# Six batches instead of five in the second group norm, the last bias additions on DVE, and new hand-written orders, in a fused convolution and attention kernel

## The chip, the cores and the metric

One core of a Trainium2 chip runs the whole program. The metric is the device time of one execution in microseconds (us). Names of engines: PE is TensorE (PEld its weight loads), DVE is VectorE, ACT is ScalarE, POOL is GpSimd, SP is SyncE, which here only issues DMAs.

## What is computed

The input x has 8 images of 128 channels and 16 x 16 pixels, all float32. The reference, cut to what matters:

```python
# stage 0, per channel
out = x + bias[None, :, None, None]
out = upsample2(out, up_filter * 2)              # separable, 12 taps, both axes
out = leaky_relu(out, 0.2) * sqrt(2)
y   = downsample2(out, down_filter)              # back to 16 x 16
# stage 1
xn  = group_norm(y, gn1_gamma, gn1_beta, 32)
q, k, v = split(qkv_w @ xn + qkv_b)              # 8 heads of 16
a   = softmax(q @ k.T / 4) @ v                   # 256 x 256 scores per head
a   = out_w @ a + out_b
a   = group_norm(a, gn2_gamma, gn2_beta, 32)
h, g = split(mlp1_w @ a)                         # 512 rows each
return y + mlp2_w @ (silu(h) * g)
```

Both group norms are taken per image, so each image's norm needs that image alone.

## The kernel before

Each of the five engines has its own straight list of steps, written out by hand, in blocks named after it. A step waits for counters (semaphores) that other engines raise, and an engine goes through its list in order, so a step that waits holds everything behind it on its engine. Nothing is scheduled at run time. Products that need float32 accuracy in one fast pass are done as three passes over a high and a low part (`three`, lines 772 to 774).

The steps that the change and the prediction touch:

- **Stage 0.** SP loads the input as windows `win` in three parts: two quarters of the batch (`in_xw`, 6 windows each of 128 x 256) and then the second half (`in_xh`, 6 windows of 128 x 512). `add_bias` adds the bias to a window in place, on DVE (line 1499) for the quarters and on POOL (line 364) for the half. PE's `upsample(n)`, n from 0 to 15, makes a quarter of the enlarged picture of two images (line 790), ACT's `leaky(n)` reads it (line 507), PE's `downsample(b)` makes image b of y (line 822) and ACT's `read_y(b)` takes its squares and sums (lines 515, 517). Upsample n needs `leaky(n - 4)`, since four PSUM banks are shared. ACT also blanks the six stacks of q and k once (`fill`, line 500, 1.9 us each).
- **First norm.** `GN1_BATCHES` has three batches of images. Of each, PE sums (`group_means`, line 806), DVE makes the variance (lines 1514 to 1517), POOL the coefficients (`first_coefficients`, lines 378 to 381), and POOL normalises image by image (`normalise`, lines 405 to 410); image 0 is done by DVE (lines 1523 to 1526).
- **Attention, image by image.** PE's `project_qk(i)` and `project_v(i)`; ACT and DVE split q and k in parts (`high_parts`, lines 524 and 525; `low_parts`, line 1531); SP copies them with six DMAs into the stacks (`stack(i)`, line 311). PE's `maxima(i, h, c)` (line 862) makes scores from which DVE's `reduce_max(i, h)` (line 1548) takes row maxima; `turn_maxima(i)` turns them, ACT's `read_rows(i)` reads them, and SP's `rows(i)` (line 317) copies them in as a row. Then PE's `scores(i, h, c)` (line 888), ACT's `exponentials(i, h)` (line 531), PE's `weigh` (line 913, 32 matmuls an image), and a chain that normalises and projects: `read_sums`, `merge`, `turn_sums`, `invert`, `spread_inverse`, `turn_inverse`, `normalise`, `project_out`, `read_proj`, `square_attn`.
- **Second norm.** `GN2_BATCHES` is [(0, 2), (2, 4), (4, 6), (6, 7), (7, 8)]. For each batch: `group_means` on PE, `read_means` on DVE (line 1505), `second_coefficients` on POOL (lines 388 to 394), then `second_norm(i)` on POOL (lines 447 to 452).
- **MLP.** Each image has two pairs p. PE's `up_project(p, j, e)` (four calls a pair, three matmuls each), ACT's `squash(p)` (line 598, from p = 8 on line 600 with another function), DVE's `swish_value` and `gate` (lines 1580, 1597, 1593), ACT's `split_high(p)` (line 586), POOL's `split_low(p)` (line 424), PE's `down_project(p, e)` (two calls a pair, three matmuls each), DVE's `residual(i)` (line 1602), SP's `store(i)` (line 322).

PE's list mixes all of this: maxima run one to two images ahead of scores, and MLP calls are put between them.

Of the kernel before, what the change touches and what calls it, by code (L numbers as in the profile page):

```python
# [75 lines left out]
GN2_BATCHES = [(0, 2), (2, 4), (4, 6), (6, 7), (7, 8)]  # L76
# [4 lines left out]
def build(nc, xw, xh, factors, vecs, wqk, wv, wo, w1, w2,  # L81
          ident, gmat, swap, out):
    ctx = ExitStack()
    with ctx:
# [131 lines left out]
        biased_dve, biased_pool = sem("biased_dve"), sem("biased_pool")  # L216
# [65 lines left out]
        def _(sp):  # L282
# [51 lines left out]
            stack(5)  # L334
            stack(6)
            rows(4)
            rows(5)
            stack(7)
            rows(6)
            store(0)  # L340
            store(1)
            rows(7)
# [6 lines left out]
        def _(pool):  # L349
# [9 lines left out]

            def add_bias(t):  # L360
                pool.wait_ge(fac_in, 16)
                pool.wait_ge(win_in[t][2], 16)
                x4 = win_at(t, 2, 2).rearrange("p (b c) -> p b c", c=C)
                pool.tensor_tensor(x4, x4, bias_bc[:, None, :].to_broadcast([128, B // 2, C]), ALU.add).then_inc(biased_pool, 1)  # L364
# [90 lines left out]
            for j in range(0, 5):  # L455
                add_bias(j)
# [3 lines left out]
            add_bias(5)  # L460
            first_coefficients(1)
            normalise(2)
            normalise(3)
            split_w2()
            split_w1()
            first_coefficients(2)
# [3 lines left out]
            second_norm(0)  # L470
            second_norm(1)
            split_low(0)
            second_coefficients(4)
            second_norm(2)
            second_norm(3)
            for j in range(1, 4):
                split_low(j)
            second_coefficients(5)
            second_norm(4)
            split_low(4)  # L480
            split_low(5)
            second_norm(5)
            split_low(6)
            second_coefficients(6)
            second_norm(6)
            for j in range(7, 10):
                split_low(j)
            second_coefficients(7)
            split_low(10)
# [5 lines left out]
        def _(act):  # L495
# [116 lines left out]
            leaky(6)  # L612
            fill(2, 0)
            for j in range(7, 10):
                leaky(j)
            read_y(2)
            high_parts(0)
            leaky(10)
            fill(2, 1)
            read_y(3)  # L620
            read_early_v(0)
# [4 lines left out]
            read_y(4)  # L626
            read_early_v(1)
            leaky(15)
            high_parts(2)
            read_y(5)  # L630
            read_y(6)
            read_rows(0)
            read_y(7)
            read_early_v(2)
            sum_biases()
            exponentials(0, 0)
            exponentials(0, 1)
            high_parts(3)
            for j in range(2, 6):
                exponentials(0, j)  # L640
            read_rows(1)
            exponentials(0, 6)
# [6 lines left out]
            exponentials(1, 2)  # L649
            spread_inverse(0)  # L650
            for j in range(3, 6):
                exponentials(1, j)
            read_rows(2)
            read_proj(0)
            exponentials(1, 6)
            square_attn(0)
            exponentials(1, 7)
            read_sums(1)
            exponentials(2, 0)
            exponentials(2, 1)  # L660
            high_parts(5)
            spread_inverse(1)
            for j in range(2, 6):
                exponentials(2, j)
            read_proj(1)
            read_rows(3)
            square_attn(1)
            exponentials(2, 6)
            exponentials(2, 7)
            read_sums(2)  # L670
            exponentials(3, 0)
            exponentials(3, 1)
            high_parts(6)
            exponentials(3, 2)
            exponentials(3, 3)
            spread_inverse(2)
            for j in range(4, 7):
                exponentials(3, j)
            read_rows(4)
            exponentials(3, 7)  # L680
            squash(0)
            read_proj(2)
            square_attn(2)
            read_sums(3)
            split_high(0)
            high_parts(7)
            exponentials(4, 0)
            spread_inverse(3)
            squash(1)
            for j in range(1, 4):  # L690
                exponentials(4, j)
            read_proj(3)
# [3 lines left out]
            square_attn(3)  # L696
            exponentials(4, 6)
            exponentials(4, 7)
            split_high(1)
            squash(2)  # L700
# [3 lines left out]
            exponentials(5, 2)  # L704
            exponentials(5, 3)
            split_high(2)
            exponentials(5, 4)
            spread_inverse(4)
            exponentials(5, 5)
            exponentials(5, 6)  # L710
            read_rows(6)
            exponentials(5, 7)
            squash(3)
            read_proj(4)
            square_attn(4)
            split_high(3)
            read_sums(5)
            exponentials(6, 0)
            exponentials(6, 1)
            squash(4)  # L720
            exponentials(6, 2)
            spread_inverse(5)
            for j in range(3, 6):
                exponentials(6, j)
            read_proj(5)
            exponentials(6, 6)
            square_attn(5)
            exponentials(6, 7)
            split_high(4)
            squash(5)  # L730
            read_rows(7)
            split_high(5)
            read_sums(6)
            exponentials(7, 0)
            squash(6)
            exponentials(7, 1)
            exponentials(7, 2)
            spread_inverse(6)
            exponentials(7, 3)
# [730 lines left out]
        def _(dve):  # L1470
# [269 lines left out]
            for j in range(11, 14):  # L1740
                gate(j)
# [68 lines left out]
```

## Time and profile before

| | us |
|---|---|
| median of 3 runs (146.26 to 147.64) | 147.03 |
| the profiled execution, its own time | 146.93 |
| span of the profiled execution | 145.1 |
| PE busy | 138.5 (95%) |
| ACT busy | 104.5 (72%) |
| DVE busy | 88.2 (61%) |
| POOL busy | 75.2 (52%) |

The clock that PE was granted is 1.0 of full speed (2.4 GHz) in all 40 slices of the page. A busy time counts from start to modelled end of overlapping instructions, so it overstates: what an engine can do per microsecond is read from starts of instructions that follow each other without a wait.

### The profile page before, as it was taken

Reading aid. Unit: us, or ns where it says so; the run is one execution under the profiler, and the core shown is the slowest. Engines: PE = TensorE matmul, PEld = TensorE weight load, DVE = VectorE, ACT = ScalarE, POOL = GpSimd, SP = SyncE. Lnnn points to the kernel's source line nnn. Section 1 sums busy time; section 2 is a strip of 40 time slices with the busy share of each in tenths; the row PEclk is TensorE's granted clock in tenths of the full one; section 3 lists DMA queues with packets and bytes.
Section 4 is the critical chain, followed back from the end, with each engine's and each line's share of the span. In section 5 each row is a group of like instructions: output and inputs, shape, how many; then the busy total and the mean of one; then the engine's idle time right before and its main releaser. Section 6 shows DMA issues by size and latency. Waiting matters only on the chain.

```text
span 145.1 us, 3307 instructions
## 1 busy us (share of the span) xinstructions
PE 138.5 (95%) x1150; PEld 122.2 (84%) x1150; DVE 88.2 (61%) x187; ACT 104.5 (72%) x235; POOL 75.2 (52%) x126
## 2 busy tenths in 40 slices
PE   6999888999999999999999999999999999999992
PEld 5899578999988687788896998797997997999891
DVE  1940133077649679699699889768684715634251
ACT  6956997955448688697793996894995995766330
POOL 7008985066584850402840304892108988589930
PEclk9999999999999999999999999999999999999999
DMA  3999200746530061331606103501001010011012
GB/s 110 285 272 338 91 0 15 205 113 185 178 113 0 10 169 49 106 113 42 182 0 175 53 0 85 138 0 38 0 7 38 0 43 0 0 41 36 0 36 72
DMA packets 12368, 12.12 MB, mean 83 GB/s; under 512 B 1600, under 2 KB 11328, under 8 KB 12352
## 3 DMA queue, kind: packets, MB, share of 16 engines
q1 hardware_dynamic: 12208, 11.81, 27.4%
q8 instruction: 9, 0.15, 0.4%
q10 hardware_dynamic: 144, 0.10, 0.2%
q14 instruction: 7, 0.06, 0.1%
HBM read 4.50 MB, written 1.05 MB: 38 GB/s over the span
## 4 chain that ended last, share of the span: by engine, by line
PE 63%; SPq 10%; POOL 9%; DMA 7%; issue 4%; DVE 3%; POOLq 1%; ACT 1%; ACTq 0%
PE ps L888 10%; PE po L913 10%; PE pm L862 9%; SPq L311 6%; SPq L286 4%; DMA win<-in_xh 4%; PE pf L772 3%; PE pf L774 3%; PE pf L773 3%; PE px L772 3%; POOL gated_lo L424 3%; PE po L936 3%; PE px L774 2%; PE px L773 2%; POOL win L364 2%
## 5 line engine op out<-in xcount | busy, mean ns | idle before, releaser
L1548 DVE TENSOR_REDUCE neg_max<-pm 128x2 f32<-128x512 f32 x64 | 42.3, 683 | 11.8 <-PE pm L862 11.2
L531 ACT ACTIVATE up_t<-ps 128x512 f32<-128x512 f32 x64 | 36.0, 595 | 4.6 <-PE ps L888 2.5
L888 PE MATMUL ps<-q_stack,k_stack 128*128 128x256 f32 x128 | 27.6, 302 | 0.0
L862 PE MATMUL pm<-k_stack,q_stack 127*128 127x256 f32 x128 | 26.3, 300 | 0.3 <-DVE neg_max L1548 0.2
L424 POOL TENSOR_TENSOR gated_lo<-win,gated_hi 128x512 fp32r<-128x512 f32 x14 | 18.1, 1304 | 12.6 <-ACT gated_hi L586 12.6
L888 PEld LDWEIGHTS ps<-q_stack,k_stack 128*128 128x128 f32 x128 | 19.5, 189 | 2.3 <-ACT up_t L531 1.0
L862 PEld LDWEIGHTS pm<-k_stack,q_stack 127*128 127x128 f32 x128 | 19.1, 189 | 2.5 <-DVE neg_max L1548 1.0
L913 PE MATMUL po<-up_t,v_aug 128*32 128x256 f32 x256 | 15.7, 382 | 0.0
L772 PE MATMUL pf<-xm_hi,w_hi 128*128 128x256 f32 x44 | 13.4, 304 | 0.3 <-issue 0.3
L586 ACT ACTIVATE gated_hi<-win 128x512 fp32r<-128x512 f32 x14 | 8.8, 631 | 6.6 <-DVE win L1597 4.4
L773 PE MATMUL pf<-xm_lo,w_hi 128*128 128x256 f32 x44 | 12.3, 280 | 0.0
L774 PE MATMUL pf<-xm_hi,w_lo 128*128 128x256 f32 x44 | 12.3, 279 | 0.0
L388 POOL TENSOR_TENSOR sq<-gs 128x2 f32<-128x2 f32 (+1 forms) x5 | 1.0, 195 | 21.2 <-DVE gs L1505 21.2
L913 PEld LDWEIGHTS po<-up_t,v_aug 128*32 128x32 f32 x256 | 7.6, 109 | 5.0 <-issue 0.2
L364 POOL TENSOR_TENSOR win<-win,fac 128x512 f32<-128x512 f32 x6 | 7.5, 1275 | 8.3 <-DMA win<-in_xh 8.3
L772 PEld LDWEIGHTS pf<-xm_hi,w_hi 128*128 128x128 f32 x44 | 8.3, 189 | 1.3 <-issue 1.3
L790 PE MATMUL pf<-win,up_w 128*128 128x256 f32 x32 | 8.1, 386 | 0.9 <-ACT up_t L507 0.9
L1531 DVE SCALAR_TENSOR_TENSOR qk_parts<-px,vec,qk_parts 128x256 fp32r<-128x256 f32 x16 | 6.9, 470 | 2.9 <-ACT qk_parts L525 2.9
L549 ACT ACTIVATE early<-po,vec 128x256 f32<-128x256 f32 x8 | 3.8, 474 | 6.6 <-PE po L913 6.6
L773 PEld LDWEIGHTS pf<-xm_lo,w_hi 128*128 128x128 f32 x44 | 8.3, 189 | 0.0
L790 PE MATMUL ps<-win,up_w 128*128 128x256 f32 x32 | 8.3, 400 | 0.0
L774 PEld LDWEIGHTS pf<-xm_hi,w_lo 128*128 128x128 f32 x44 | 8.3, 188 | 0.0
(149 smaller groups left out, 344.6 us busy)
## 6 DMA issues: line engine op xcount, KB each, us to landing
q_stack<-qk_parts SPq DMA_DIRECT2D x24, 128.0 KB, 2.4
k_stack<-qk_parts SPq DMA_DIRECT2D x24, 128.0 KB, 2.4
win<-in_xw SPq DMA_DIRECT2D x12, 128.0 KB, 3.2
win<-in_xh SPq DMA_DIRECT2D x6, 256.0 KB, 5.5
out<-win SPq DMA_DIRECT2D x8, 128.0 KB, 1.7
win<-in_w SPq DMA_DIRECT2D x1, 512.0 KB, 3.7
w_s<-in_w SPq DMA_DIRECT2D x1, 256.0 KB, 3.6
wqk_s<-in_wqk SPq DMA_DIRECT2D x1, 128.0 KB, 4.1
```

The lines of the kernel that those rows point to most:

```text
L364: pool.tensor_tensor(x4, x4, bias_bc[:, None, :].to_broadcast([128, B // 2, C]), ALU.add).then_inc(biased_pool, 1)
L424: pool.tensor_tensor(gated_lo[:, r, :], gated[:, r, :], gated_hi[:, r, :].bitcast(F32), ALU.subtract).then_inc(gated_split, 1)
L531: act.activation(probs[:, h // HALF, h % HALF, :, :].rearrange("p c n -> p (c n)"), ps[:, h % 2, :], ACT.Exp, scale=D ** -0.5).then_inc(pr ...
L586: act.activation(gated_hi[:, r, :], gated[:, r, :], ACT.Copy).then_inc(gated_hi_ready, 1)
L772: pe.matmul(dst, w_hi, x_hi, start=start, stop=False)
L773: pe.matmul(dst, w_hi, x_lo, start=False, stop=False)
L774: return pe.matmul(dst, w_lo, x_hi, start=False, stop=stop)
L790: mm = pe.matmul(up_bank[n % 4][:, j * Q:(j + 1) * Q], up_w[:, UP_WEIGHT_OF[m], :, :].rearrange("p a b -> p (a b)"), win_at(t, q), start=T ...
L862: return pe.matmul(pm[:, h % 2, c * N:(c + 1) * N], stack_rows(q_stack, i, slice(0, TOP))[:, h, c * 128:(c + 1) * 128], stack_rows(k_stack ...
L888: return pe.matmul(ps[:, h % 2, c * N:(c + 1) * N], stack_rows(k_stack, i, slice(0, TOP + 1))[:, h, c * 128:(c + 1) * 128], stack_rows(q_s ...
L913: mm = pe.matmul(po[32 * g:32 * g + 32, 0, half * N:(half + 1) * N], v_aug[:, i % V_RING, c, half, b + 32 * g:b + 32 * g + 32], probs[:, h ...
L1548: dve.tensor_reduce(neg_max[:, i % 2, 2 * h:2 * h + 2], pm[:, h % 2, :].rearrange("p (c n) -> p c n", c=2), AX.X, ALU.max, negate=True).th ...
```

## The change

Four things are changed, and they come together:

1. `GN2_BATCHES` begins with two batches of one image instead of one batch of two, so there are six batches. This adds one `group_means`, one `read_means` and one `second_coefficients`.
2. The bias of the second half of the input is added by DVE (six instructions of 128 x 512) instead of POOL, and PE's upsamples wait for DVE's counter for all three parts.
3. SP: the load of w1 is put ahead of the second stack, and some rows and stores change places.
4. The lists of PE, ACT, DVE and POOL are written in new orders, from `upsample(5)` to `up_project(13)` on PE.

```diff
-GN2_BATCHES = [(0, 2), (2, 4), (4, 6), (6, 7), (7, 8)]
+GN2_BATCHES = [(0, 1), (1, 2), (2, 4), (4, 6), (6, 7), (7, 8)]
...
             stack(0)
+            load_w1()
             stack(1)
-            load_w1()
+            rows(0)
             stack(2)
-            rows(0)
             rows(1)
             stack(3)
+            stack(4)
             rows(2)
-            stack(4)
             rows(3)
...
-            def add_bias(t):
-                pool.wait_ge(fac_in, 16)
-                pool.wait_ge(win_in[t][2], 16)
...
-                    if q < 2:
-                        pe.wait_ge(biased_dve, NWIN * q + t + 1)
-                    else:
-                        pe.wait_ge(biased_pool, t + 1)
+                    pe.wait_ge(biased_dve, NWIN * min(q, 2) + t + 1)
...
             def add_bias(t, q):
+                n = 1 if q < 2 else 2
                 dve.wait_ge(win_in[t][q], 16)
...
+                dve.tensor_tensor(x4, x4, bias_bc[:, None, :].to_broadcast([128, n * B // QUARTERS, C]), ALU.add).then_inc(biased_dve, 1)
```

Where steps are moved, the order of an engine's instructions tells more than the diff. Lines of the changed kernel are 6 to 12 lower than those of before. First ACT in stage 0, from `leaky(5)` on: `up_t` is written by leaky, `q_stack` and `k_stack` by fill, `y` by read_y, `qk_parts` by high_parts. Before:

```order
L507 ACTIVATE up_t<-ps 128x2x256
L500 ACTIVATE q_stack<-rest 128x2048
L500 ACTIVATE k_stack<-rest 128x2048
L507 ACTIVATE up_t<-pf 128x2x256
L500 ACTIVATE q_stack<-rest 128x2048
L507 ACTIVATE up_t<-pf 128x2x256
L507 ACTIVATE up_t<-ps 128x2x256 x2
L515 ACTIVATE y_squares,mv<-pm 128x256
L517 ACTIVATE y,mv<-pm 128x256
L524 ACTIVATE qk_parts<-px,vec 128x256
```

And the same place of the change:

```order
L498 ACTIVATE up_t<-ps 128x2x256
L491 ACTIVATE q_stack<-rest 128x2048
L491 ACTIVATE k_stack<-rest 128x2048
L498 ACTIVATE up_t<-pf 128x2x256 x2
L498 ACTIVATE up_t<-ps 128x2x256 x2
L506 ACTIVATE y_squares,mv<-pm 128x256
L508 ACTIVATE y,mv<-pm 128x256
L491 ACTIVATE q_stack<-rest 128x2048
L515 ACTIVATE qk_parts<-px,vec 128x256
L516 ACTIVATE qk_parts<-px,vec 128x256
```

The fill of the third q stack stood between leaky(6) and leaky(7) and now stands behind read_y(2).

Second, PE around the first image's output projection and the first call of the MLP, in the change (`L924` is `project_out`, `L794` the group means, `L864` turn_maxima, `L901` weigh, `pf<-xm_hi` up_project):

```order
L794 MATMUL po<-mv,gmat_s 128x2
L850 MATMUL pm<-k_stack,q_stack 128x256
L864 MATMUL pm<-ident_s,neg_max 128x128
L901 MATMUL po<-up_t,v_aug 32x256 x8
L850 MATMUL pm<-k_stack,q_stack 128x256 x4
L832 MATMUL px<-wv_s,win 128x128 x2
L901 MATMUL po<-up_t,v_aug 32x256 x8
L850 MATMUL pm<-k_stack,q_stack 128x256 x4
```

In the order of before, the first group means of the second norm (`L806`, with 4 columns for two images) stand one image later, next to the third weigh:

```order
L844 MATMUL px<-wv_s,win 128x128 x2
L862 MATMUL pm<-k_stack,q_stack 128x256 x2
L806 MATMUL po<-mv,gmat_s 128x4
L862 MATMUL pm<-k_stack,q_stack 128x256 x2
L913 MATMUL po<-up_t,v_aug 32x256 x16
```

So the first up_project stands ahead of scores(2, 0, 0) in the change, and ahead of scores(3, 4, 0) before; by the third weigh (image 2), PE has run 8 of the MLP's calls in the change and none before.

Third, POOL at the end: before, one `split_low` stands between the last coefficients and the last norm.

```order
L394 TENSOR_SCALAR shift<-shift_t,vec 128x1
L424 TENSOR_TENSOR gated_lo<-win,gated_hi 128x512
L447 TENSOR_SCALAR up_t<-up_t,scale,shift 128x256
L449 TENSOR_SCALAR xm_hi<-up_t,scale,shift 128x256
L452 TENSOR_TENSOR xm_lo<-up_t,xm_hi 128x256
```

In the change it stands ahead of those coefficients:

```order
L418 TENSOR_TENSOR gated_lo<-win,gated_hi 128x512 x3
L382 TENSOR_TENSOR sq<-gs 128x1
L383 TENSOR_TENSOR sq<-gs,sq 128x1
L384 TENSOR_SCALAR ve<-sq 128x1
L385 TENSOR_TENSOR rstd<-ve,half_neg 128x1
L386 TENSOR_SCALAR scale<-rstd,vec 128x1
L387 TENSOR_TENSOR shift_t<-gs,scale 128x1
L388 TENSOR_SCALAR shift<-shift_t,vec 128x1
L441 TENSOR_SCALAR up_t<-up_t,scale,shift 128x256
```

On PE at that place, four calls of the MLP (two of up_project 8 and both of down_project 6) have moved from behind weigh(7) to ahead of it, and three of up_project 10 from behind project_out(7) to ahead of it.

## Rows read from the trace of the kernel before

**Rows 1.** The page: busy time, share of the span and instructions of each engine.

```profile
PE 138.5 (95%) x1150; PEld 122.2 (84%) x1150; DVE 88.2 (61%) x187; ACT 104.5 (72%) x235; POOL 75.2 (52%) x126
```

**Rows 2.** Busy time by stretch, us from the start; engines as named.

```profile
43.00:70.00 27.00, 26.50 (x243) 21.27 (x244) 21.37 (x44) 20.46 (x49) 10.48 (x23) 1.00 0.26 73
70.00:119.00 49.00, 48.79 (x454) 43.40 (x454) 37.97 (x75) 40.10 (x97) 24.15 (x40) 1.00 0.18 51
```

**Rows 3.** Timeline 11 to 23: start, us, engine, line, tiles, [idle before <- releaser].

```profile
11.49 6.19 POOL L364 TENSOR_TENSOR win<-win,fac 128x512 f32<-128x512 f32 x5 [8.29 <-DMA win<-in_xh]
...
15.77 0.16 DVE L1514 TENSOR_SCALAR gs<-po 128x2 f32<-128x2 f32 x1 [4.59 <-PE po L806]
...
17.64 0.42 POOL L355 TENSOR_SCALAR wqk_hi<-wqk_s 128x256 fp32r<-128x256 f32 x1
17.84 0.59 ACT L507 ACTIVATE up_t<-pf 128x512 f32<-128x512 f32 x1
...
18.32 1.91 ACT L500 ACTIVATE q_stack<-rest 128x2048 fp32r<-128x2048 f32 x1
...
18.48 1.13 PE L790 MATMUL pf<-win,up_w 128*128 128x256 f32 x4 [0.92 <-ACT up_t L507]
...
18.83 0.72 POOL L378 TENSOR_TENSOR rstd<-ve,half_neg 128x2 f32<-128x2 f32 x1
...
22.27 0.36 PE L772 MATMUL px<-xn_hi,wqk_hi 128*128 128x256 f32 x1 [0.83 <-DVE xn_lo L1526]
```

**Rows 4.** The chain that ended last, weigh of images 0 (half), 1, 2, 3 and 7.

```profile
48.05 1.00 PE po L913 x16
...
58.60 1.86 PE po L913 x32
...
67.73 1.93 PE po L913 x32
...
78.03 1.86 PE po L913 x32
...
119.62 1.86 PE po L913 x32
```

**Rows 5.** DVE's timeline, instructions that follow each other without a wait.

```profile
54.66 1.29 DVE L1548 TENSOR_REDUCE neg_max<-pm 128x2 f32<-128x512 f32 x2
55.87 0.41 DVE L1575 TENSOR_TENSOR weighted<-po,merged 128x256 f32<-128x256 f32 x1
...
84.23 0.67 DVE L1580 SCALAR_TENSOR_TENSOR win<-win,pf 128x512 f32<-128x512 f32 x1
84.83 0.68 DVE L1548 TENSOR_REDUCE neg_max<-pm 128x2 f32<-128x512 f32 x1
```

**Rows 6.** PE's timeline, three-pass products that follow each other without a wait.

```profile
118.02 0.28 PE L774 MATMUL pf<-xm_hi,w_lo 128*128 128x256 f32 x1
...
118.25 0.28 PE L773 MATMUL pf<-xm_lo,w_hi 128*128 128x256 f32 x1
```

**Rows 7.** SP's timeline: the first two of a stack's six copies.

```profile
58.63 1.17 SPq L311 DMA_DIRECT2D q_stack<-qk_parts  x2
```

**Rows 8.** The chain that ended last, from the last group means on.

```profile
129.00 0.30 PE po L806 x2
...
132.04 1.27 POOL gated_lo L424
...
134.48 0.74 POOL xm_lo L452
...
142.58 0.42 DVE win L1602
```

**Rows 9.** ACT's timeline, behind weigh of image 7.

```profile
122.24 0.47 ACT L550 ACTIVATE early<-po,vec 128x256 f32<-128x256 f32 x1
122.72 1.28 ACT L600 ACT_TABLE_LOAD   x1
124.02 0.60 ACT L600 ACTIVATE win<-pf 128x512 f32<-128x512 f32 x1
```

More of the change, by code:

```diff
@@ L611, in _ @@
             fill(1, 1)
-            leaky(6)
-            fill(2, 0)
-            for j in range(7, 10):
+            for j in range(6, 10):
                 leaky(j)
             read_y(2)
+            fill(2, 0)
             high_parts(0)
@@ L695, in _ @@
             exponentials(4, 5)
-            square_attn(3)
+            spread_inverse(3)
             exponentials(4, 6)
             exponentials(4, 7)
-            split_high(1)
-            squash(2)
+            split_high(2)
+            read_proj(3)
+            square_attn(3)
+            split_high(3)
             exponentials(5, 0)
@@ L1035, in _ @@
             maxima(0, 3, 1)
-            project_v(1)
-            upsample(15)
+            downsample(5)
             maxima(0, 4, 0)
@@ L1114, in _ @@
             scores(1, 3, 1)
+            maxima(2, 5, 0)
+            maxima(2, 5, 1)
+            turn_inverse(0)
             maxima(2, 6, 0)
             maxima(2, 6, 1)
+            scores(1, 4, 0)
+            scores(1, 4, 1)
+            project_v(4)
+            project_out(0)
+            scores(1, 5, 0)
+            scores(1, 5, 1)
+            scores(1, 6, 0)
+            scores(1, 6, 1)
             maxima(2, 7, 0)
             maxima(2, 7, 1)
-            scores(1, 4, 0)
-            scores(1, 4, 1)
-            turn_inverse(0)
+            project_qk(5)
+            scores(1, 7, 0)
+            scores(1, 7, 1)
             maxima(3, 0, 0)
+            group_means(3)
             maxima(3, 0, 1)
-            scores(1, 5, 0)
-            scores(1, 5, 1)
             turn_maxima(2)
-            scores(1, 6, 0)
-            project_out(0)
-            scores(1, 6, 1)
-            project_v(4)
+            weigh(1, 0, 0)
+            weigh(1, 0, 1)
             maxima(3, 1, 0)
@@ L1134, in _ @@
             maxima(3, 2, 1)
-            scores(1, 7, 0)
-            scores(1, 7, 1)
-            weigh(1, 0, 0)
-            weigh(1, 0, 1)
+            project_v(5)
             weigh(1, 1, 0)
@@ L1143, in _ @@
             maxima(3, 4, 0)
+            maxima(3, 4, 1)
+            project_qk(6)
+            maxima(3, 5, 0)
+            maxima(3, 5, 1)
+            up_project(0, 0, 0)
+            turn_sums(1)
             scores(2, 0, 0)
@@ L1221, in _ @@
             maxima(5, 2, 0)
+            scores(3, 6, 1)
             maxima(5, 2, 1)
-            project_v(6)
-            up_project(0, 1, 0)
+            scores(3, 7, 0)
+            scores(3, 7, 1)
+            turn_inverse(2)
+            project_v(7)
             maxima(5, 3, 0)
             maxima(5, 3, 1)
-            up_project(0, 1, 1)
+            up_project(2, 1, 1)
+            maxima(5, 4, 0)
+            scores(4, 0, 0)
+            project_out(2)
+            scores(4, 0, 1)
+            maxima(5, 4, 1)
+            maxima(5, 5, 0)
+            maxima(5, 5, 1)
+            scores(4, 1, 0)
+            scores(4, 1, 1)
             weigh(3, 0, 0)
@@ L1282, in _ @@
             scores(5, 1, 1)
+            maxima(6, 3, 1)
             maxima(6, 4, 0)
             maxima(6, 4, 1)
+            group_means(5)
+            down_project(2, 0)
+            down_project(2, 1)
             maxima(6, 5, 0)
@@ L1299, in _ @@
             maxima(6, 7, 1)
-            down_project(0, 1)
             scores(5, 4, 0)
```

624 lines of the change are left out of this document (302 added, 322 removed).

## The prediction, written before the change was run

> **What bounds the kernel now.** I read the page's busy shares first. PE is busy 138.5 of 145.1 us, ACT 104.5, DVE 88.2 [rows 1], at full clock. So PE's own work sets the time, and only what makes PE wait can be won. The work of PE is all but the same in the change, so the questions are where it waits now, which waits go, and which come.
>
> The view by stretch shows that the busy share hides much of it. From 43 to 70 us PE counts 26.5 of 27.0 us busy and DVE 21.4 [rows 2], but busy time is counted to modelled ends, which overlap. The starts tell more. Three-pass products follow each other at (118.25 - 118.02) / 2 = 0.115 us although one lasts 0.28 [rows 6]. So I priced the list of PE with such distances: 0.118 (rounded up) for a product of 256 columns (maxima and scores one each, up_project and down_project three each), 1.86 for the weigh of an image [rows 4], and estimates from like rows for the few others (project_qk six products, 0.7; project_v, the turns and the output projection 1.2 together).
>
> In the chain that ended last, the weigh of image 0 starts at 48.0, that of image 3 at 78.0 and that of image 7 at 119.6 [rows 4]. Between the first two PE has 50 scores, 54 maxima, 12 weigh calls (5.6), three or four each of the small things and 4 MLP calls: 25.9 us of work in 30.0. Between the last two it has 39.3 us in 41.6. The second stretch has MLP calls between the attention's and loses 2.3 in 39.3, 6%. This 6% I take as what switching between kinds of matmul costs anyway. At 6% the first stretch would take 27.5, so **it loses 2.5 us more than it need**. Its DVE work, priced likewise (a reduction 0.60, since two take 55.87 - 54.66 = 1.21; swish and gate 0.60 by 84.83 - 84.23 [rows 5]), is 25 reductions and 8.6 us of others, 23.6 in 30.0. An image without MLP gives PE about 8 us of work and DVE 7.3, so DVE is nearly as loaded as PE, and each reduction that comes late holds the next maxima.
>
> Ahead of that, the timeline of 11 to 23 us shows **two plain waits of PE**, 0.92 us for ACT's leaky(6) and 0.83 for the first normalised image [rows 3]. The first is there because two fills of 1.9 us each stand ahead of leaky(6). The second is there because POOL is adding the bias from 11.49 to 17.68, then splits wqk, and takes up the coefficients at 18.83, though DVE had begun their variance at 15.77 [rows 3].
>
> **The front.** The change moves the 6 additions (1.24 us each on POOL, 6.19 for five [rows 3]) to DVE, which has nothing to do then. DVE's price for 512 elements with an addition is not in this stretch. From below it is one swish, 0.60 a piece [rows 5]; from above, POOL's 1.24. I take 0.6, since that row has the same engine and size. Either way the input's last window lands about 15 and the sixth addition is done between 15.7 and 16.5. PE's group means now stand two upsamples later, at about 17.3 by the rate of 0.43 us a matmul, so POOL can start the coefficients at 18.0 instead of 18.83 and the image is normalised at 21.4 instead of 22.2. PE meanwhile has both downsamples to do, which no fill holds up any more (the fill between leaky(6) and leaky(7) is gone from there), and comes to project_qk(0) at 21.3 to 21.4. So both waits go: **-1.75**. Then something comes back. The third k stack's fill (1.9) and read_y(3) now stand ahead of leaky(11), for which upsample(15) waits, and upsample(15) is now ahead of the maxima. By my count leaky(11) ends at 28.5 and PE could use it at 27.6. Part of that lag would have met it later anyway, so I put +0.65: the front gives **-1.1**.
>
> Here a page speaks on the moved additions. The Trainium skill, SBUF — State Buffer, section "Who interferes with whom", says that a DVE instruction with two inputs in SBUF and a POOL instruction that reads SBUF exclude each other for the whole instruction. The trace of before cannot show it, as DVE idles while POOL adds. By the page the split of wqk would start up to one addition later. That split has 18.0 - 17.1 = 0.9 us to spare, so the sum is the same by the one and by the other.
>
> **The middle.** With image 0 a batch of its own, the first up_project can stand ahead of scores(2, 0, 0) instead of scores(3, 4, 0), some ten microseconds earlier. Between the weigh of images 0 and 3 PE now has 54 scores, 60 maxima and 12 MLP calls, 31.4 us of work, at 6% 33.3 us. DVE has 28 reductions, three swishes and gates and the rest, 29.1 us, so its load goes from 23.6 / 30.0 = 79% to 29.1 / 33.3 = 87%. The MLP gives PE 1.4 us a pair of up_projects for 1.2 of DVE, against 0.60 of DVE for 0.24 of PE in maxima, so PE has more to fill DVE's delays with, but no more slack of DVE comes from it. All of the 2.5 could go, or none. I take 1.0, because the load rises: **-1.0**. The moved work itself (5.5 us) is only brought forward.
>
> The sixth batch costs one more group_means on PE, 0.30 [rows 8], of which 0.05 overlaps: **+0.25**. Its coefficients (about 2.5 us) fall on POOL where it idles; 24.2 of 49 us are busy there [rows 2].
>
> **The end.** The last image's chain goes from the last group means at 129.0 through POOL's coefficients, a split_low of 1.27 at 132.04, and the norm, whose last piece ends at 134.48 + 0.74 = 135.2 [rows 8]. The last piece of PE's list needs it. The change takes the split_low out of the chain, which makes it 129.0 to 133.9, 4.9 us. But it also takes three MLP calls (1.05) out of the work with which PE covers the chain from project_out(7) on, and puts split_high(10) between read_proj and square_attn. PE's cover from the means on is then 0.7 + 0.7 + 1.4 + 1.4 = 4.2 against 4.9, a wait of 0.7 where it was 0.43: **+0.25**.
>
> **Sum.** -1.1 - 1.0 + 0.25 + 0.25 = -1.6. Against the profiled execution's own 146.93 us (its span 145.1 and 1.8 around it) this is **145.3**. That execution lies 0.1 below the median of 147.03, so I leave it there.
>
> **Rivals.**
> - *The middle is won whole.* What speaks for it: the late reductions of [rows 4]'s first stretch are those of images 0 to 2, where PE had nothing else to do. Then -1.1 - 2.5 + 0.5: 143.8.
> - *The front's gain stays, or the middle's, but not both.* SP now issues a stack's six copies ahead of rows(2). Two of them take 1.17 [rows 7], so all six 3.6, and the row of image 2 lands that much later; by my count scores(2, 0, 0) would wait 0.5. With such waits at two or three places (residual(1) now stands ahead of rows(6) in the same way) the middle gives nothing: 146.3.
> - *DVE becomes the bound and the kernel is slower.* Between the weigh of images 0 and 2 DVE has 21.9 us of work and PE 22.3. If DVE's order does not meet PE's, each of DVE's waits for ACT or PE is lost for good. This decides from 3.1 us more of PE's waits in that stretch than I count. At 3.5 us: 1.9 more than now, 148.8. Against it: DVE is idle for 5.6 of the 27 us from 43 to 70 [rows 2], which has room for much of the added work.
> - *The table load falls into the last chain.* The change puts squash(8), the first of the other function, ahead of read_sums(7). ACT loads its table in 1.28 us and goes on 0.02 later [rows 9]. The load fits into the 1.86 of weigh(7) [rows 4], so I count nothing. If it were one half microsecond late, the last chain would be as much later: 145.8. The Trainium skill, ScalarE: Activation LUTs, section "What ACT_TABLE_LOAD costs", gives 1.38 us of draining besides the load. By that, read_sums(7) would come 1.3 us late and the end with it, 146.6. The trace disagrees: the instruction behind the load starts at 124.02, right at its end.
>
> **How the numbers follow.** About 1% (1.5 us) is what a measurement of this kernel can tell from no change. Chances: the forecast 0.45 (144.4 to 146.0), the middle won whole 0.15, only part kept (with the table load) 0.27, DVE as the bound 0.13. Faster by over 1%, below 145.5, are the second and some 0.33 of the first: 0.48. Slower by over 1% is most of the last: 0.12. The rest is 0.40. The range reaches from the whole middle won to part kept and a bit of DVE's case: 143.8 to 147.2.
>
> **What would show it.** Right: PE's first project_qk near 21.4 without a wait; POOL's first power (rstd) near 18.0; the weigh of image 0 at 46.5 to 47; the weigh of image 7 starting at 119 to 119.5 although 1.4 us more work stands ahead of it; a PE wait of about 0.7 ahead of up_project(14). Wrong: PE waiting for DVE's maxima between 50 and 70, or for the DMA of max_row ahead of scores(2, 0, 0); reductions that wait while PE waits as well; an upsample(15) that waits over 1 us.

## The result, and the profile after

Each ratio below is this kernel over the kernel before, timed on one chip, with a 95% interval; it compares undisturbed executions alone, so it is not the quotient of the two medians.

| | median us | ratio to before |
|---|---|---|
| before | 146.84 (18 runs) | |
| the change | 147.43 (146.82 to 148.17, 18 runs) | 1.0062 [1.0041, 1.0083] |

The forecast was 145.3 in a range of 143.8 to 147.2. The change is slower than before by 0.6%, and its time lies above the range. The profiled execution of the change took 146.94 us, that of before 146.93, so the two pages look alike. The first row is of the page of the change, the two others are its view by stretch (columns as in [rows 2]).

```profile
PE 139.4 (96%) x1152; PEld 123.2 (85%) x1152; DVE 92.1 (63%) x194; ACT 104.7 (72%) x235; POOL 69.3 (48%) x127
```

```profile
43.00:70.00 27.00, 26.83 (x236) 22.59 (x235) 23.04 (x49) 21.30 (x52) 13.76 (x32) 1.00 0.32 86
70.00:119.00 49.00, 48.47 (x460) 41.90 (x459) 35.14 (x70) 38.26 (x91) 22.27 (x37) 1.00 0.20 58
```

Against [rows 2], PE is 0.33 us busier in the first stretch and 0.32 less in the second. Next comes the timeline of the front, which answers to [rows 3] (rows without a bracket did not wait).

```profile
15.83 0.40 POOL L355 TENSOR_SCALAR wqk_hi<-wqk_s 128x256 fp32r<-128x256 f32 x1 [12.63 <-DMA wqk_s<-in_wqk]
...
17.89 0.71 POOL L372 TENSOR_TENSOR rstd<-ve,half_neg 128x2 f32<-128x2 f32 x1 [0.85 <-DVE ve L1505]
...
21.31 0.36 PE L763 MATMUL px<-xn_hi,wqk_hi 128*128 128x256 f32 x1
...
27.57 1.02 PE L778 MATMUL pf<-win,up_w 128*128 128x256 f32 x4
28.43 0.28 PE L794 MATMUL po<-mv,gmat_s 128*128 128x4 f32 x2
28.60 0.74 PE L850 MATMUL pm<-k_stack,q_stack 127*128 127x256 f32 x4
```

The front looks as forecast: the power at 17.89 (18.0 was said), project_qk(0) at 21.31 without a wait (21.3 to 21.4). The upsample at 27.57 is the sixteenth, and it did not wait either, though 0.65 had been charged for it. Then the chain that ended last, the weighs of images 0 to 7 (the first two in halves), as [rows 4]:

```profile
45.43 1.00 PE po L901 x16
...
56.81 1.07 PE po L901 x16
...
71.18 1.86 PE po L901 x32
...
80.92 1.93 PE po L901 x32
...
91.94 1.86 PE po L901 x32
...
100.51 1.86 PE po L901 x32
...
110.86 1.93 PE po L901 x32
...
120.68 1.86 PE po L901 x32
```

Image 0 is 2.6 us ahead of before, image 7 is 1.1 behind. That alone isn't a loss, as the change has 8 MLP calls done by image 2 where before had none. So I counted **lost time**. For each matmul of PE, it is the distance to the next start less the usual distance of that pair of kinds (the lower quartile in the trace of before). Profiles differ by chance in the front, so the table takes a second profile of each kernel (r_before and r_after below, which took 146.20 and 147.47, somewhat further apart than the ratio says). The MLP calls of a stretch are counted in PE's list.

| stretch | before: us, MLP calls, lost | change: us, MLP calls, lost |
|---|---|---|
| start to weigh(0) | 47.3, 0, 6.56 | 45.8, 0, 5.44 |
| weigh(0) to (1) | 10.6, 0, 1.71 | 11.5, 0, 2.20 |
| (1) to (2) | 9.2, 0, 1.61 | 14.3, 8, 1.57 |
| (2) to (3) | 10.2, 4, 1.13 | 9.8, 4, 0.93 |
| (3) to (4) | 12.1, 8, 0.71 | 11.0, 10, 0.90 |
| (4) to (5) | 9.1, 8, 0.80 | 8.6, 6, 1.20 |
| (5) to (6) | 10.8, 12, 0.97 | 10.4, 10, 1.26 |
| (6) to (7) | 9.6, 12, 0.82 | 9.8, 10, 1.68 |
| weigh(7) to the end | 23.0, 52, 1.58 | 21.9, 48, 1.82 |
| sum | lost 15.9, last matmul ends 141.83 | lost 17.0, last matmul ends 143.08 |

The front gives 1.12, the stretches of images 0 to 3 lose 0.25 more than before, those of images 3 to 7 lose **1.74** more, and the end 0.24. That is 1.11, and with some 0.15 for the added group means (28.43 to 28.60 above) it is the 1.25 between the two ends. In the late stretches PE also has less to do: 41.56 less 3.30 is 38.3 us of work in before, 39.72 less 5.04 is 34.7 in the change. Of 3.6 us of work that are gone from there only 1.8 came off the time.

A pair of kinds that before lacks has no usual distance of its own, so single rows of the table are soft by a few tenths. Counting work alone is a second way. From weigh(3) to (7) the change has 12 products of MLP calls, four maxima, four scores and the six products of project_qk(7) fewer, 26 x 0.118 = 3.1 us, and one project_v of 0.45. That is 3.5 us less work in 1.84 less time, so 1.7 more lost, as in the table. From weigh(0) to (1) the two ways differ: the stretch is 0.91 longer, for four more products (0.47), one group means (0.22 to the next start) and a turn (some 0.1, an estimate from the turn at 46.84, which is followed at 46.92). That leaves 0.1, where the table has 0.5.

The lost times between the weighs hardly vary from execution to execution: the change's first profile has 2.20, 1.59, 0.94, 0.89, 1.22, 1.24 and 1.65.

### The profile page after: what moved, and what is told of

It reads as the page before. It is cut to its first block, busy times and chain, and to the rows that moved or that the text cites. A ratio compares the mean times of both kernels' runs of the same rounds, so it can differ in the third digit from the quotient of the medians.

```text
span 145.1 us, 3317 instructions
## 1 busy us (share of the span) xinstructions
PE 139.4 (96%) x1152; PEld 123.2 (85%) x1152; DVE 92.1 (63%) x194; ACT 104.7 (72%) x235; POOL 69.3 (48%) x127
## 4 chain that ended last, share of the span: by engine, by line
PE 89%; ACT 4%; DVE 3%; issue 2%; ACTq 0%
PE pm L850 11%; PE po L901 11%; PE ps L876 10%; PE pm L810 4%; PE pf L763 4%; PE ps L778 4%; PE px L763 4%; PE pf L778 4%; PE pf L765 3%; PE pf L764 3%; PE px L764 3%; PE px L765 3%; PE px L832 3%; PE po L810 3%; PE pf L810 2%
## 5 line engine op out<-in xcount | busy, mean ns | idle before, releaser
L876 PE MATMUL ps<-q_stack,k_stack 128*128 128x256 f32 x128 | 26.9, 304 | 0.0
L850 PE MATMUL pm<-k_stack,q_stack 127*128 127x256 f32 x128 | 25.5, 299 | 0.1
L901 PE MATMUL po<-up_t,v_aug 128*32 128x256 f32 x256 | 15.9, 383 | 0.4 <-DVE gs L1493 0.3
L901 PEld LDWEIGHTS po<-up_t,v_aug 128*32 128x32 f32 x256 | 7.8, 109 | 5.1 <-issue 0.8
L1487 DVE TENSOR_TENSOR win<-win,fac 128x256 f32<-128x256 f32 (+1 forms) x18 | 8.9, 512 | 2.3 <-DMA win<-in_xh 1.4
L372 POOL TENSOR_TENSOR rstd<-ve,half_neg 128x2 f32<-128x2 f32 (+1 forms) x3 | 2.4, 808 | 12.4 <-DVE ve L1505 12.4
L810 PE MATMUL pm<-dn_w,up_t 128*128 128x128 f32 (+2 forms) x64 | 7.8, 278 | 0.2 <-ACT up_t L498 0.2
L810 PEld LDWEIGHTS pm<-dn_w,up_t 128*128 128x128 f32 x64 | 7.5, 192 | 0.4 <-ACT up_t L498 0.4
```

What stands on the lines that cost most here:

```text
L810: mm = pe.matmul(down_bank(b)[:, o0 * W:o1 * W], up_at(m, b), dn_w[:, o0 - 2 * m + 3:o1 - 2 * m + 3, :].rearrange("p a b -> p (a b)"), sta ...
L850: return pe.matmul(pm[:, h % 2, c * N:(c + 1) * N], stack_rows(q_stack, i, slice(0, TOP))[:, h, c * 128:(c + 1) * 128], stack_rows(k_stack ...
L876: return pe.matmul(ps[:, h % 2, c * N:(c + 1) * N], stack_rows(k_stack, i, slice(0, TOP + 1))[:, h, c * 128:(c + 1) * 128], stack_rows(q_s ...
L901: mm = pe.matmul(po[32 * g:32 * g + 32, 0, half * N:(half + 1) * N], v_aug[:, i % V_RING, c, half, b + 32 * g:b + 32 * g + 32], probs[:, h ...
L1487: dve.tensor_tensor(x4, x4, bias_bc[:, None, :].to_broadcast([128, n * B // QUARTERS, C]), ALU.add).then_inc(biased_dve, 1)
```

## Experiments

### Where the loss is: front and late orders apart

Theories at the start: A, the front's gain is real and orders behind it lose it; B, a chain that doesn't depend on the front absorbs it; C, DVE's six additions cost something.

**e_bias**, the kernel before with part 2 of the change alone:

```diff
-            for j in range(0, 5):
-                add_bias(j)          (POOL; add_bias(5) further down too)
+            add_bias(0, 2)           (DVE, and five more)
```

> The kernel before, with one part of the change alone: the bias of the second half is added by DVE, and nothing is reordered. Theory A (the front's gain is real, and the new orders behind it lose it again between the sixth weigh and the last norm): POOL can take up the first coefficients at about 17.1 instead of 18.83, the wait ahead of project_qk(0) shrinks by most of its 0.8 to 1.0 us, the end comes 0.5 to 1.0 us earlier. Theory B (the attention that follows is held by its own chain through DVE, ACT and the DMAs, so what the front wins is absorbed wherever it is won): PE reaches project_qk(0) earlier, and the end moves by less than 0.3 us. Theory C (DVE's additions cost the others something): slower by 0.3 or more.

Measured: 146.21, ratio 0.9962 [0.9929, 0.9996].

**e_front**, the whole new front on the kernel before: also `fill(2, 0)` behind `read_y(2)` and these orders on PE.

```diff
-            group_means(0)   upsample(8..10)  downsample(2)  project_qk(0)  downsample(3)  upsample(11)  project_v(0)
+            upsample(8, 9)   group_means(0)   downsample(2)  downsample(3)  project_qk(0)  upsample(10, 11)  project_v(0)
```

> The kernel before, with the change's front alone: bias on DVE, the third fill behind read_y(2), PE's upsamples 8 and 9 ahead of the group means and both downsamples ahead of project_qk(0). Everything behind it is in the old order, with five batches. Theory A: both waits of PE (2.1 us by starts) go, and the old order behind keeps it: 1.2 to 2.0 us faster, ratio 0.986 to 0.992. Theory B: the weigh of image 0 starts earlier, and the gain is gone at the end: within 0.5 us of before, ratio above 0.996.

Measured: 146.51, ratio 0.9975 [0.9944, 1.0007].

**e_oldfront**, the change with the old front (both of the above undone).

> The changed kernel, with the front put back: bias on POOL, the third fill and the order of PE's first downsamples as before. All behind it is the change's. Theory A: the two waits of 0.9 and 1.0 us are back and go through to the end: 1.3 to 2.0 us slower than the change, ratio to before about 1.015. Theory B: the same as the change within 0.5 us, ratio 1.004 to 1.008.

Measured: 148.74, ratio 1.0122 [1.0080, 1.0164].

**e_late**, the change with three things moved in its late part:

```diff
 ACT: read_proj(5)
-     split_high(5)  square_attn(5)
+     square_attn(5)  split_high(5)
 PE:  up_project(6, 0, 1)
-     up_project(6, 1, 0)  up_project(6, 1, 1)  group_means(6)
+     group_means(6)  up_project(6, 1, 0)  up_project(6, 1, 1)
 PE:  scores(7, 3, 1)
-     down_project(6, 0)  down_project(6, 1)
      turn_inverse(6)  ...  up_project(7, 1, 1)
+     down_project(6, 0)  down_project(6, 1)
      group_means(7)
```

> The changed kernel with three places late in it reordered: ACT takes the squares of image 5 before split_high(5), the group means ahead of weigh(6) stand two MLP calls earlier, and down_project(6) stands right ahead of the group means of image 6, which wait for ACT's squares. Theory A: PE's waits of 0.48 ahead of weigh(6) and 0.61 ahead of these means shrink to under 0.1 each, and the end comes 0.5 to 1.0 us earlier than in the change, ratio to before 0.999 to 1.003. Theory B: the waits go and come back as a longer one ahead of up_project(14), since the last image's chain sets the end: within 0.3 us of the change.

Measured: 147.74, ratio 1.0044 [1.0011, 1.0077].

Behind the old front the change's other parts are 1.2% slower than before, behind the new one 0.6%, so they cost some 1.8 us and the front covers part of it: A in kind. C falls, the additions on DVE cost nothing. The front alone is worth little on the old orders (0.2 to 0.4%), which speaks for a part of B. e_late took away the wait of 0.61 ahead of the seventh group means, and that of 0.35 ahead of weigh(6), and gained nothing that stands clear of the noise: weigh(5) to (6) takes 10.45 there and 10.43 in the change. In its timeline PE waits in another place of the same stretch, since down_project(6) no longer stands ahead of turn_inverse(6):

```profile
117.07 0.44 PE L919 MATMUL po<-ident_s,inv_wide 128*128 128x128 f32 x2 [0.56 <-ACT inv_wide L548]
```

The lost time from weigh(6) to weigh(7) is 1.69 there, 1.65 in the change. A wait that moves when a filler moves suggests that filler is short, not that it stands wrong.

### The sixth batch, and the old orders put behind the new ones

**h_six**, e_front with the six batches; image 0's group means stand right ahead of `weigh(1, 0, 0)`, image 1's where the old pair's stood, POOL and DVE accordingly.

> The kernel before with the change's front, and with the six batches: image 0's group means stand right ahead of image 1's weigh, image 1's where those of both images stood, and everything else keeps the old order. Theory D (the sixth batch costs its own instruction and little more): 0.25 to 0.5 over the kernel with the new front alone, so a ratio to before of 0.998 to 1.002. Theory E (the batch itself is what spoils the change, by a wait of PE for image 0's squares ahead of weigh(1) and by the longer chain of coefficients): over 1 us more, 1.005 or above.

Measured: 148.02, ratio 1.0112 [1.0081, 1.0143].

The batch costs 1.4% over e_front there (1.0112 over 0.9975). The timeline of PE at weigh(1) shows why:

```profile
58.93 0.35 PE L817 MATMUL po<-mv,gmat_s 128*128 128x2 f32 x2
60.02 0.85 PE L924 MATMUL po<-up_t,v_aug 128*32 128x256 f32 x11 [0.74 <-DVE gs L1523]
```

and the row of DVE between them:

```profile
58.53 1.28 DVE L1566 TENSOR_REDUCE neg_max<-pm 128x2 f32<-128x512 f32 x2
59.73 0.15 DVE L1523 TENSOR_SCALAR gs<-po 128x2 f32<-128x2 f32 x1
```

The means lie in the bank that the weigh writes, so DVE must read them first, and DVE had two reductions ahead. The stretch from weigh(0) to weigh(1) loses 2.89 instead of 1.74, that from (3) to (4) 1.06 instead of 0.72. Ahead of weigh(0) it lost 1.55 more too, in large part by the front's chance (below). The change puts one maxima and a turn between its means and the weigh. In the change's repeat DVE's read ends at 57.15 and weigh(1) starts at 57.30, 0.15 behind it as in h_six (59.88 to 60.02). But the turn ahead of it starts at 57.03 only, so this hand-over costs under 0.27. By these two places, what a batch costs besides its instruction goes by what DVE has ahead of its read: 1.15 us of lost time in h_six.

**h6**, the change's lists up to weigh(6), then what is left in the order of before.

> The change's orders up to image 6's weigh, then the order of before for all that is left. It keeps the wait ahead of image 6's weigh and takes out the change's last 30 us. Theory A: the waits ahead of the seventh group means (0.61) and of up_project(14) (0.74 against 0.4) go, so 0.5 to 1.0 less than the change, ratio to before 1.000 to 1.003. Theory F: the cover that was used early is missing, and waits of the same sum turn up elsewhere behind the cut: 1.004 to 1.008.

Measured: 147.98, ratio 1.0109 [1.0070, 1.0149]. The wait ahead of up_project(14) fell to 0.38 and the end lost 1.56 instead of 1.83, but the stretch from weigh(6) to (7), for which six MLP calls were left instead of ten, lost 2.65.

**h3**, the same with the cut at weigh(3).

> The change's orders on every engine up to image 3's weigh, and the order of before for all that is left. Theory A (the change is ahead by 1.8 to 2.3 us of work there and the late orders lose it): the end stays ahead of the change by 1 us or more, ratio to before 0.985 to 0.997, unless the stretch without MLP calls right behind the cut loses the same. Theory F (the middle order only moved cover forward, and whoever takes MLP calls early pays later): the stretch between the weighs of images 3 and 4 or 4 and 5 now has stalls of 2 us or more where before had 0.7 to 0.8, and the ratio is 1.000 to 1.008.

Measured: 156.73, ratio 1.0694 [1.0655, 1.0734]. Most of the loss is none of the theories': PE waited once for the row of image 4, whose copy SP issued behind the six copies of image 6's stack, in the timeline:

```profile
82.08 0.60 SPq L317 DMA_DIRECT2D q_stack<-max_row  x1
84.06 0.58 PE L899 MATMUL ps<-q_stack,k_stack 128*128 128x256 f32 x1 [4.60 <-DMA q_stack<-max_row]
```

**h3b**, h3 with `rows(4)` ahead of `stack(6)` on SP.

> As the kernel that had the change's orders up to image 3's weigh and the old ones behind it, but with SP keeping the change's order through the row of image 4, so that this row's copy no longer stands behind the six copies of image 6's stack (PE waited 4.8 us for it there). If that alone made the 10 us: stall between the weighs of images 2 and 3 back from 6.9 to 0.9. Theory F (calls of the MLP are the cover of the late images, and those brought forward are missing later) then expects 2 us or more of stalls between the weighs of images 3 and 5, where PE has nearly no MLP calls left, and 0.8 to 1.0 in each stretch behind them, as before has: ratio 1.000 to 1.015. Theory A (the late orders are bad by themselves): 0.990 to 1.000.

Measured: 149.95, ratio 1.0255 [1.0223, 1.0286], so that SP's order alone made 6.8 us of h3's time. From weigh(3) to (4), where no MLP call was left, PE loses 4.78, the longest by this wait:

```profile
85.60 0.41 PE L935 MATMUL po<-swap_s,dens 128*128 128x128 f32 x2 [1.75 <-DVE merged L1578]
```

Behind it, with the old orders and the old number of calls, the stretches lose 0.75, 0.99 and 0.80, just as before. So nothing that the change's middle leaves behind is bad in itself: what a stretch loses goes by what stands in it. And calls taken early are missing somewhere.

**e_front2**, e_front with `upsample(12)` ahead of `project_v(0)` and `upsample(14)` ahead of `project_qk(1)`.

> The kernel before with the change's front, and with upsample(12) moved ahead of project_v(0) and upsample(14) ahead of project_qk(1), as the change has them. If the two waits seen there (0.43 and 0.39) are PE coming too early, they shrink to under 0.1 each and the time is 0.4 to 0.8 below before's: ratio 0.992 to 0.997. If the chain through ACT and POOL sets project_qk(1) and the first maxima anyway, it stays at 0.9975.

Measured: 146.60, ratio 0.9987 [0.9960, 1.0013]. The two small waits became one of 0.93 ahead of the first maxima.

### The front in repeated profiles

**r_before** and **r_after**, both kernels once more.

> The kernel before once more, for a second look at the spread of its front. In the profiles so far PE's first upsamples run at the slow pace (0.43 us a record) until 4.3 to 6.9 us, and the later the pace doubles, the later the kernels with the new front reach image 0's weigh (45.4 to 46.4 in the change's orders). Theory G (the two waits of the old front absorb this): weigh(0) at 47.7 to 48.2 here whatever the pace does. Otherwise it moves with it, up to 48.9.

> The change once more. Theory G: image 0's weigh starts between 45.3 and 46.4, by when the pace doubles, and nothing behind it takes this up: image 7's weigh is 75.2 to 75.4 later and the span follows. The same stalls as in the first profile between the weighs (2.2, 1.6, 0.9, 0.9, 1.2, 1.2, 1.65), each within 0.1.

Measured, one execution each: 146.20 and 147.47. Rows of the timeline of the repeat of before, which answer to [rows 3]:

```profile
10.33 6.19 POOL L364 TENSOR_TENSOR win<-win,fac 128x512 f32<-128x512 f32 x5 [7.13 <-DMA win<-in_xh]
...
19.01 1.13 PE L790 MATMUL pf<-win,up_w 128*128 128x256 f32 x4 [1.09 <-ACT up_t L507]
...
21.77 0.37 PE L772 MATMUL px<-xn_hi,wqk_hi 128*128 128x256 f32 x1
```

POOL's first addition starts 1.16 us earlier than in the first profile, as its window landed earlier, and **the wait of 0.83 ahead of project_qk(0) is not there**. The wait for leaky(6) is (1.09). PE's own pace varies as well. These are the first upsamples of PE in that repeat and in e_front:

```profile
4.32 2.90 PE L790 MATMUL ps<-win,up_w 128*128 128x256 f32 x8
```

```profile
4.31 1.98 PE L777 MATMUL ps<-win,up_w 128*128 128x256 f32 x8
```

The same eight records start 0.43 us apart at first and 0.22 later. The doubling came between 4.2 and 7.0 us in the 16 profiles, and by it these eight records take from 1.8 us (h3) to 3.1 (a_cover). Theory G fell for before: weigh(0) came at 47.26, 0.4 ahead of its bounds. For the change it held, 45.84 with the stretches behind it unchanged.

All profiles but one have another number in common. From the first product of project_qk(0) to the first maxima it is 7.29 us in before (22.27 to 29.56), 7.39 in its repeat, 7.29 and 7.31 in the change, 7.34 in e_front and e_front2. The exception is e_oldfront (8.19). It has the work of before there and the sixteenth upsample besides, and since PE does not wait, that upsample makes it 0.86 longer. Elsewhere PE has other work in these 7.3 us or it waits (in e_front2 0.79 for the first k stack), so a front on the old orders gains only what project_qk(0) comes earlier: at 21.8 in both repeats, nothing. In the change it gains since it has one more upsample done by the first maxima (four records, 0.86), and that is nearly all of the 1.12.

### Is the late loss missing work beside a fixed chain?

**a_cover**, the change with its down projections shifted: one pair fewer between weigh(3) and (4), one more behind weigh(6).

```diff
 PE: group_means(5) [images 2, 3]
-    down_project(2, 0)  down_project(2, 1)      (and each later pair one slot later)
 PE: weigh(6, 1, 1)
+    down_project(4, 0)  down_project(4, 1)
     scores(7, 0, 0)  ...  turn_sums(6)  scores(7, 3, ..)
     down_project(6, 0)  down_project(6, 1)  turn_inverse(6)
```

DVE's residual(1), SP's row of image 6 and ACT's split_high(6) move with them.

> The change with its down-projection calls shifted later so that two fewer (of ten) stand between the weighs of images 2 and 4 and two more (twelve, as in the kernel before) between those of images 6 and 7; DVE's second residual, SP's row of image 6 and one ACT piece follow. Theory F: the stretch from weigh(3) to weigh(4) gets 0.7 us shorter with its stall unchanged (0.9), and the stall between weigh(6) and weigh(7) falls from 1.65 to 0.8 to 1.0, so 0.6 to 0.8 us less than the change in all, ratio to before 0.999 to 1.003. If the late waits come from an order that is wrong and not from missing cover, they stay and the ratio is that of the change, 1.004 to 1.008.

Measured: 148.33, ratio 1.0140 [1.0108, 1.0172]. That was worse than the change, against theory F. Image 6's chain, from its weigh to the end of its squares, is 8.35 us in the repeat of before (109.22 to 117.57) and 8.43 in that of the change, but 9.60 here. One reason is in the timeline: down_project(6), ahead of turn_inverse(6), now waits for its split.

```profile
117.59 0.39 PE L780 MATMUL px<-gated_hi,w_hi 128*128 128x256 f32 x1 [0.38 <-POOL gated_lo L422]
```

PE is a link of this chain (turns, projection), so work put ahead of its links lengthens it.

**a_cover2**, the same number of calls, but each slot in the chain kept and the two extra calls right ahead of the means:

```diff
     up_project(7, 1, 1)
+    down_project(6, 0)  down_project(6, 1)      (the slots of 5 and 6 hold 4 and 5)
     group_means(7)
```

residual(2) and split_high(6) stand a little later than in a_cover.

> The change with two MLP calls fewer ahead of image 4's weigh and two more between the weighs of images 6 and 7, but placed so that none comes into the chain of image 6: the calls that stand early in that stretch keep their slots (one number lower), and the two extra ones stand right ahead of the seventh group means, where PE waited 0.61. In both kernels the squares of image 6 end 8.35 to 8.45 us after its weigh starts. Theory H (PE waits because its own work in that stretch is shorter than this chain): the 8.4 stay, the wait of 0.61 is gone, the stretch grows by 0.1 to 0.3 only though it has 0.70 more work, and its stall falls from 1.68 to 1.0 to 1.3. The stretch from weigh(3) to weigh(4) gets 0.2 shorter as in the last try, so the whole is level with the change: ratio to before 1.004 to 1.010. Against it: the chain gets longer too, as in the last try (9.6), and the ratio is 1.011 or above.

Measured: 147.78, ratio 1.0049 [1.0012, 1.0085]. The timelines, first of the repeat of the change, then of a_cover2: weigh(6), the last record of its squares, and the seventh group means.

```profile
111.38 1.93 PE L901 MATMUL po<-up_t,v_aug 128*32 128x256 f32 x32 [0.35 <-DVE gs L1493]
...
119.61 0.20 ACT L563 ACTIVATION_READ_ACCUMULATOR y_squares<-up_t 128x1 f32 x1
...
119.95 0.35 PE L794 MATMUL po<-mv,gmat_s 128*128 128x2 f32 x2 [0.46 <-ACT y_squares L563]
```

```profile
111.78 1.93 PE L918 MATMUL po<-up_t,v_aug 128*32 128x256 f32 x32 [0.35 <-DVE gs L1517]
...
120.01 0.20 ACT L567 ACTIVATION_READ_ACCUMULATOR y_squares<-up_t 128x1 f32 x1
...
120.45 0.28 PE L811 MATMUL po<-mv,gmat_s 128*128 128x2 f32 x2
```

The chain is 8.43 in both, and 0.70 us more work fitted into the same 9.77 us from weigh(6) to weigh(7): the lost time fell from 1.68 to 0.97. Theory H holds. In the change PE's own work beside the chain is shorter than the chain, and PE waits the rest. The whole didn't get faster, because the pair taken out between weigh(3) and (4) was cover there too: that stretch lost 1.38 instead of 0.90 and got only 0.2 us shorter.

**r_bias**, e_bias once more.

> The kernel before with nothing changed but that DVE adds the bias of the second half, once more. The first comparison had it 0.4% below before, with an interval that ended at 0.9996. Theory I (POOL's late additions are a chance wait: they start when the first window of the second half lands, 11.49 in the profile of before, 10.33 in its repeat, and cost PE 0.83 us in the one and nothing in the other): 0 to 0.5% below before, and project_qk(0) at 21.7 to 21.9 by when the pace doubles. Otherwise it is the 0.8 us that the first profile showed, a ratio of 0.9945 or below.

Measured: 146.11, ratio 0.9958 [0.9923, 0.9993]. With the first comparison that is twice 0.4% faster than before. The additions on DVE alone are the one part of the change whose interval lies below 1, both times narrowly; e_front (0.9944 to 1.0007) can't be told apart from it. The ratio lies where theory I expects it. That the gain is an average over executions with and without the wait is argued, not shown. Its project_qk(0) came at 20.99, 0.7 ahead of what it says; the pace of PE had doubled at once in that execution.

## Why the prediction was wrong

**The step that failed** is "This 6% I take as what switching between kinds of matmul costs anyway". It made a constant of the time lost between images 3 and 7, and the sum has no term for it. The lost time there is, in part, what PE's work falls short of each image's chain, and the change takes 3.6 us of work out of exactly these stretches: four of 40 MLP calls, four maxima, four scores and the projections of image 7. It went from 3.30 to 5.04, **+1.74** where nothing was charged. a_cover2 shows the mechanism at one place. That it is the same at the others is inferred from the table and the count of work, and it goes by all of PE's work, not by calls alone: from weigh(3) to (4) the change has two calls more, but four maxima, four scores and image 7's projections fewer, and loses 0.2 more.

**The middle, forecast -1.0**, is +0.25 (4.45 lost before, 4.70 after). MLP calls beside images 1 and 2 were to fill DVE's delays. They took little off: 0.2 from weigh(2) to (3). From weigh(1) to (2) the loss stayed at 1.6 though 8 calls were added, and weigh(0) to (1), with the new batch in it, lost 0.5 more by the table and 0.1 by the count of work. The 2.5 us "more than it need" came from the same constant of 6%.

**The front, forecast -1.1**, is -1.12 between the repeats, but by luck: two errors cancel. The -1.75 counted two waits of [rows 3]; the one of 0.83 was chance of that execution. The +0.65 for upsample(15) never came, as that upsample did not wait. In the pair of first profiles the front is -2.28, since before was unlucky there and the change lucky, and this is why the two profiled executions tie at 146.9.

**The sixth batch, forecast +0.25.** Its instruction is 0.15 to 0.2. The step did not name the hand-over: the weigh waits until DVE has read the means. With it weigh(0) to (1) loses over 1 us more in h_six; in the change it costs under 0.27, so the term was about right. In the change a wait for the read shows ahead of weigh(6) as well, where the means of images 4 and 5 stand right ahead of the weigh, the 0.35 above; e_late, without it, was no shorter there.

**The end, forecast +0.25**, is +0.24. The wait ahead of up_project(14), forecast 0.7, as PE's row:

```profile
135.31 0.36 PE L763 MATMUL pf<-xm_hi,w_hi 128*128 128x256 f32 x1 [0.58 <-issue]
```

It starts 0.74 later than usual.

**The signs.** The power, project_qk(0) and the wait of 0.7 came as said in the first profile. weigh(0) was said at 46.5 to 47 and came at 45.4 and 45.8; weigh(7) was said at 119 to 119.5 and came at 120.6 and 121.2, and that is where the forecast fell.

**The rivals.** The forecast time of none came out. DVE as the bound, the slower one, has the right sign by another mechanism: PE did wait where work was short, but late, not between weigh(0) and (3). SP's order did no harm in the change, as scores(2, 0, 0) did not wait; h3 shows what it can cost (4.6 us in one wait). The table load came on ACT ahead of the sums and cost next to nothing. On ACT's timeline, which answers to [rows 9]:

```profile
121.29 1.28 ACT L591 ACT_TABLE_LOAD   x1
122.59 0.60 ACT L591 ACTIVATE win<-pf 128x512 f32<-128x512 f32 x1
123.08 0.47 ACT L540 ACTIVATE early<-po,vec 128x256 f32<-128x256 f32 x1
```

The sums start 2.47 us after weigh(7) starts, against 2.30 in before. The next instruction follows the load by 0.02 us again, and ACT's instruction ahead of it ended at 121.27. So no draining of 1.38 us, as the Trainium skill has it (ScalarE: Activation LUTs, "What ACT_TABLE_LOAD costs"), stands beside a load here.

The price of DVE's addition was taken as 0.6; three take 2.06 us, 0.69 each, and since DVE had nothing else, it did not matter. Whether additions on DVE hold POOL's split back, as the prediction's page on SBUF would have it, no run shows: the split waited for its own load (15.83) and the last addition was over (13.45 + 2.06 = 15.51).

## What to carry over

When work is the filler beside a chain that repeats, count filler per repetition before and after: what is brought forward is missing later, and a busy share or a constant share of loss doesn't show it. Filler helped only behind everything that the chain itself needed of that engine (a_cover against a_cover2). A wait seen in one profile of a kernel's first microseconds may be chance; a second profile of the same kernel tells, and 0.8 us of a forecast of 1.6 stood on one.

## What the runs showed of the hardware

- PE's pace in the first upsamples doubled at a time between 4.2 and 7.0 us that differed from execution to execution. Ahead of it PE had run eight warm-up matmuls from 1.17 us on and gone on without a gap. The granted clock showed 1.00, the level of 2.4 GHz, over these stretches in the ten profiles where I read it, though a distance of 0.43 instead of 0.22 is a factor of two, that between the levels 1.2 and 2.4 GHz. The Trainium skill (TensorE: Matmul & The Clock Gate, "What's actually happening") says that the count of slow matmuls at the start varies from run to run, and the traces agree (4.2 to 7.0).
- A row's copy behind six stack copies on SP came 4.1 us after the first of them (77.98 to 82.08) and landed in time for a matmul at 84.06, 2.0 us from its issue at most.
